# A local-attention and feed-forward kernel: score matmuls spread over both row halves and all column quarters, the down projection moved one slot on, and a new order on VectorE

## What is computed

```python
for i in range(DEPTH):                                   # 6
    x = attn_layer(shift_tokens(x), Wqkv[i], q_scale[i], k_scale[i], Wo[i]) + x
    x = ffn_layer(shift_tokens(x), ln_g[i], ln_b[i], W1[i], b1[i], W2[i], b2[i]) + x

# attn_layer: 16 heads of 64, window 32
q = l2norm(q) * qs ; k = l2norm(k) * ksc                 # then rotary with a scale
# local_attention: each window of 32 queries sees its own and the previous 32 keys
sim = einsum('bhwie,bhwje->bhwij', bq, bk2) * 8.0
attn = softmax(where(mask, -max, sim), -1)
out = einsum('bhwij,bhwje->bhwie', attn, bv2)

# ffn_layer: LayerNorm, 128 -> 2 x 341, a * gelu(gate), 341 -> 128
```

## Time and profile before

| what | us |
|---|---|
| median of three runs | 1690.2 (1688.54 to 1695.42) |
| the profiled execution | 1690.94 |
| its span, first to last instruction | 1689.1 |
| PE busy | 1604.0 (95%) |
| VectorE busy | 1461.7 (87%) |
| ScalarE busy | 1413.0 (84%) |
| GpSimd busy | 1312.3 (78%) |

### The profile page before, as it was taken

The page is one execution under the profiler, slowest core; times in us unless marked ns, Lnnn a source line. Parts: engine busy times, 40 slices in busy tenths (PEclk is TensorE's granted clock), DMA queues, the critical chain, the costliest instruction groups (busy, mean ns, idle before and its releaser), DMA issues.

```text
span 1689.1 us, 68758 instructions
## 1 busy us (share of the span) xinstructions
PE 1604.0 (95%) x25970; PEld 1294.4 (77%) x25970; DVE 1461.7 (87%) x3011; ACT 1413.0 (84%) x2851; POOL 1312.3 (78%) x1305
## 2 busy tenths in 40 slices
PE   7879999999999999999999999999999999999995
PEld 5667887777777778787777877777777777777773
DVE  4399998998899899889989989988998998889884
ACT  3267898988888898898888889888888988988885
POOL 6088888888788788888878888887888877777765
PEclk9799999999999999999999999999999999999997
DMA  4011111111111111111111111111111101110000
GB/s 150 31 43 40 36 38 38 31 45 31 53 34 31 37 37 39 50 36 33 31 37 43 48 39 31 33 31 50 45 36 37 31 28 39 40 33 26 28 24 26
DMA packets 41426, 66.40 MB, mean 39 GB/s; under 512 B 7072, under 2 KB 16032, under 8 KB 41376
## 3 DMA queue, kind: packets, MB, share of 16 engines
q1 hardware_dynamic: 40224, 65.38, 12.9%
q10 hardware_dynamic: 1152, 0.34, 0.1%
HBM read 20.61 MB, written 1.05 MB: 13 GB/s over the span
## 4 chain that ended last, share of the span: by engine, by line
PE 56%; ACT 28%; issue 10%; DVE 5%; ACTq 1%; DMA 0%; POOL 0%; DVEq 0%; POOLq 0%
PE ps_qs L530 12%; PE ps_q L530 8%; PE ps_a L530 7%; PE ps_tk L530 7%; PE ps_po L530 6%; PE ps_f L530 6%; PE ps_k L530 4%; PE ps_v L530 4%; ACT p_bd L942 4%; ACT L1052 3%; ACT L1049 3%; ACT prob L986 3%; ACT squares L948 3%; ACT q_t L942 3%; PE ps_po L650 2%
## 5 line engine op out<-in xcount | busy, mean ns | idle before, releaser
L419 POOL TENSOR_TENSOR qk<-qk,qk_rot 128x512 f32<-128x512 f32 x384 | 483.6, 1280 | 0.0
L427 POOL TENSOR_TENSOR qk<-qk,rnorm 128x512 f32<-128x512 f32 x384 | 393.0, 1044 | 77.2 <-DVE rnorm L1283 76.7
L434 POOL TENSOR_TENSOR prob<-prob,row_inv 128x512 f32<-128x512 f32 x192 | 200.4, 1044 | 152.7 <-DVE row_inv L1300 152.5
L1263 DVE TENSOR_REDUCE ssq<-squares 128x8 f32<-128x512 f32 x384 | 261.2, 680 | 3.6 <-ACT squares L948 3.4
L530 PE MATMUL ps_qs<-k_t,q_t 64*32 64x64 f32 x12224 | 210.5, 218 | 9.5 <-ACT ps_qs L942 9.4
L942 ACT COPY p_bd<-ps_po 64x512 f32<-64x512 f32 x378 | 217.1, 574 | 2.3
L530 PEld LDWEIGHTS ps_qs<-k_t,q_t 64*32 64x32 f32 x12224 | 179.8, 107 | 37.2 <-issue 27.8
L530 PEld LDWEIGHTS ps_po<-p_bd,v_back 128*64 128x64 f32 x3056 | 161.7, 137 | 46.0 <-issue 31.8
L530 PE MATMUL ps_po<-p_bd,v_back 128*64 128x64 f32 x3056 | 192.8, 225 | 0.0
L530 PE MATMUL ps_po<-p_bd,v_own 128*64 128x64 f32 x3056 | 188.5, 222 | 0.0
L530 PE MATMUL ps_a<-attn_t,wo_sb 128*64 128x257 f32 x1536 | 187.8, 386 | 0.0
(11 more groups left out here) (237 smaller groups left out, 4125.3 us busy)
## 6 DMA issues: line engine op xcount, KB each, us to landing
v_back<-v_own SPq DMA_DIRECT2D x192, 192.0 KB, 2.4
w_raw<-in_wqkv SPq DMA_DIRECT2D x48, 192.0 KB, 2.3
v_back<-v_own SPq DMA_DIRECT2D x96, 64.0 KB, 2.1
wo_sb<-in_wo SPq DMA_DIRECT2D x12, 256.0 KB, 3.0
w_sb<-in_w SPq DMA_DIRECT2D x6, 341.0 KB, 3.2
w_sb<-in_w SPq DMA_DIRECT2D x6, 192.0 KB, 2.7
x_in<-in_x SPq DMA_DIRECT2D x4, 256.0 KB, 4.4
out<-s_out SPq DMA_DIRECT2D x8, 128.0 KB, 1.9
```

Of the source, the lines that this page charges most:

```text
L419: nc.gpsimd.tensor_tensor(qk[:, s, i, :], qk[:, s, i, :], qk_rot[:, s, i, :], ALU.add).then_inc(added, 1)
L427: nc.gpsimd.tensor_tensor(heads(qk[:, s, i, :]), heads(qk[:, s, i, :]), rnorm[:, s, 8 * i:8 * i + 8].unsqueeze(2).to_broadcast([P, 8, HEAD ...
L434: nc.gpsimd.tensor_tensor(heads(prob[:, s, :]), heads(prob[:, s, :]), row_inv[:, s, :].unsqueeze(2).to_broadcast([P, 8, HEAD]), ALU.mult). ...
L1263: V.tensor_reduce(ssq[:, s, 8 * i:8 * i + 8], heads(squares[:, s, OCTET * i:OCTET * i + OCTET]), AX, ALU.add).then_inc(ssq_done, 1)
```

## The change

Three things are changed together.

**Scores in two banks.** `ps_q` and `ps_k` become halves of one two-bank tensor `ps_proj`, and `ps_qs` and `ps_tk` halves of another, `ps_score`. The scores of the first head of each pair go to the first bank and those of the second head to the second bank, 256 columns each. The column place is now `64 * odd + 32 * near`, where `near` tells two head pairs apart, so eight matmuls in a row use eight different pieces. `lay_mask` writes into both banks and therefore also waits for `k_turned`; the transposes of k wait for `sub_done`.

**Down projection.** `ff_down` moves from slot 1 (bank `ps_tk`) to slot 2, into columns 2 to 258 of the LayerNorm bank `ps_a`. The residual addition `after_ff` on VectorE moves from slot 2 to slot 3, and PE's wait for it moves from the transposes of slot 2 to the output projection of slot 3.

**VectorE's order.** The three Newton operations, the sums and the products are interleaved so that dependent operations are not neighbours. The last Newton operation, which writes `rnorm`, now stands behind the cosine product of q.

```diff
-        ps_q, ps_k, ps_v, ps_qs, ps_tk, ps_po, ps_a, ps_f = (
-            bank(n) for n in ("ps_q", "ps_k", "ps_v", "ps_qs", "ps_tk", "ps_po", "ps_a", "ps_f"))
+        ps_proj, ps_score = (ctx.enter_context(nc.psum_tensor(n, [P, 2, 512], F32)) for n in ("ps_proj", "ps_score"))
+        ps_q, ps_k, ps_qs, ps_tk = ps_proj[:, 0, :], ps_proj[:, 1, :], ps_score[:, 0, :], ps_score[:, 1, :]
+        ps_v, ps_po, ps_a, ps_f = (bank(n) for n in ("ps_v", "ps_po", "ps_a", "ps_f"))
+        ps_down = ps_a[:, TILES:TILES + SHIFTED]
...
-                ps, read = ((ps_qs, sub_done), (ps_tk, k_turned))[i]
-                wait(pe, read, u)
-                turn_into(ps, u, i, s)
+                wait(pe, sub_done, u)
+                turn_into((ps_qs, ps_tk)[i], u, i, s)
...
-                for c in range(PAIRS):
+                for far in range(2):
                     for half in range(2):
-                        g = 2 * c + half
+                        g = 2 * far + half
                         for odd in range(2):
                             w = 2 * half + odd
-                            for head in range(2):
-                                rows = slice(64 * head, 64 * head + 64)
-                                at = 64 * odd + WINDOW * head
-                                last = mm(ps[at:at + WINDOW, 64 * g:64 * g + 64],
...
+                            for near in range(2):
+                                c = 2 * far + near
+                                for head in range(2):
+                                    rows = slice(64 * head, 64 * head + 64)
+                                    at = 64 * odd + WINDOW * near
+                                    last = mm(ps[at:at + WINDOW, head, 64 * g:64 * g + 64],
...
-            def ff_down(u, m):
-
-                pe.wait_ge(k_turned, u + 1)
-                down_into(ps_tk, m)
+            def ff_down(m):
+
+                pe.wait_ge(centered, m + 3)
+                down_into(ps_down, m)
...
-                        if j == 2 and live_batch(n - 4):
-                            pe.wait_ge(x_ready, BATCHES + n - 3)
...
                     if j == 3:
                         if live_batch(n - 3):
                             ff_up(n - 3, 2)
+                        if live_batch(n - 4):
+                            pe.wait_ge(x_ready, BATCHES + n - 3)
                         if live_batch(n - 1):
                             out_projection(n - 1, 0)
                     if live(u - 4):
                         values(u - 4, n - 1, j, j % 2)
-                    if j == 1 and live_batch(n - 4):
-                        ff_down(u - 2, n - 4)
+                    if j == 2 and live_batch(n - 4):
+                        ff_down(n - 4)
...
                 act.wait_ge(q_turned, u + 1)
-                copy(ps_qs[:], mask_b[:, tile, :]).then_inc(mask_laid, 1)
+                act.wait_ge(k_turned, u + 1)
+                copy(ps_score[:, :, 0:OCTET // 2], mask_b[:, tile, :].rearrange("p (a b) -> p a b", a=2)).then_inc(mask_laid, 1)
...
-                    if j == 2 and live_batch(n - 4):
+                    if j == 3 and live_batch(n - 4):
                         after_ff(n - 4)
                     if j == 3 and live_batch(n - 2):
                         ln_var(n - 2)
                     if live(u - 3):
                         softmax_shift(u - 3, (j - 3) % 2)
                     if live(u - 1):
-                        newton(u - 1, (j - 1) % 2, u - 2)
+                        newton_half(u - 1, (j - 1) % 2)
                     sum_squares(u, 0, j % 2)
-                    rotate(n, j, 0)
+                    if live(u - 1):
+                        newton_square(u - 1, (j - 1) % 2)
+                    rotate_cos(n, j, 0)
+                    if live(u - 1):
+                        newton_finish(u - 1, (j - 1) % 2, u - 2)
+                    rotate_sin(n, j, 0)
                     if live(u - 3):
-                        sums(u - 3, (j - 3) % 2)
-                    rotate(n, j, 1)
+                        row_sums(u - 3, (j - 3) % 2)
                     sum_squares(u, 1, j % 2)
+                    if live(u - 3):
+                        invert_sums(u - 3, (j - 3) % 2)
+                    rotate_cos(n, j, 1)
+                    rotate_sin(n, j, 1)
```

More of the change, by code:

```diff
@@ L665, in project, with scores @@
                 mm(ps[:], xs_lo[:, toks], w_hi[:, cols], False, True).then_inc(done, 1)
-            def scores(u, j, s, ps=ps_qs, laid=True):
+            def scores(u, j, s, ps=ps_score, laid=True):
                 octet, tile = j // 2, j % 2
@@ L671, in scores @@
                 pe.wait_ge(k_turned, u + 1)
-                if ps is ps_qs and laid:
+                if laid:
                     pe.wait_ge(mask_laid, u + 1)
@@ L826, in drain @@
                 turn_into(ps_q, c, 0, 0)
-                pe.wait_ge(k_turned, c)
-                turn_into(ps_tk, c, 1, 0)
+                pe.wait_ge(k_scaled, END)
+                turn_into(ps_k, c, 1, 0)
                 out_projection(LAST - 1, 1)
[L830 to L834, removed]
+                pe.wait_ge(sub_done, b + 1)
+                turn_into(ps_qs, d, 0, 1)
+                scores(c, 2, 0, ps_proj, False)
+                turn_into(ps_tk, d, 1, 1)
                 values(a, LAST, 0, 0)
                 ln_spread(LAST - 2, END)
-                turn_p(b, 1, ps_tk)
+                pe.wait_ge(v_copied, END)
+                turn_p(b, 1, ps_v)
                 ln_mean(LAST - 1)
-                pe.wait_ge(sub_done, b + 1)
-                scores(d, 3, 1, ps_qs, False)
+                scores(d, 3, 1, ps_score, False)
                 ff_up(LAST - 2, 0)
@@ L847, in drain @@
                 ff_up(LAST - 2, 2)
-                values(c, LAST, 2, 0, ps_tk)
+                values(c, LAST, 2, 0, ps_k)
                 out_projection(LAST, 0)
-                turn_p(d, 1, ps_k)
+                turn_p(d, 1, ps_tk)
                 ln_spread(LAST - 1, END + 1)
@@ L1253, in rotate, with rotate_sin @@
                 cos = table[:, span(at, HEAD)]
-                sin = table[:, span(at + TILES * HEAD, HEAD)]
                 V.tensor_tensor(heads(qk[:, s, i, :]), heads(ps[:]),
                                 cos.unsqueeze(1).to_broadcast([P, 8, HEAD]), ALU.mult)
+            def rotate_sin(n, j, i):
+                s = j % 2
+                tile = j % 2
+                ps, scaled = ((ps_q, q_scaled), (ps_k, k_scaled))[i]
+                at = n // BATCHES * (4 * TILES * HEAD) + (2 * i * TILES + tile) * HEAD
+                sin = table[:, span(at + TILES * HEAD, HEAD)]
                 V.tensor_tensor(halves(qk_rot[:, s, i, :]), halves(ps[:])[:, :, ::-1, :],
@@ L1272, in clamp_unit, with newton_half @@
                 clamp(s)
-            def newton(c, s, used):
+            def newton_half(c, s):
                 dve.wait_ge(rn_started, c + 1)
@@ L1278, in newton, with newton_square, newton_finish @@
                                        op0=ALU.mult, op1=ALU.mult).then_inc(rn_step, 1)
+            def newton_square(c, s):
                 dve.wait_ge(rn_step, 2 * c + 1)
                 V.tensor_tensor(rn_b[:, s, :], rn_a[:, s, :], rn_0[:, s, :], ALU.mult).then_inc(rn_step, 1)
+            def newton_finish(c, s, used):
                 dve.wait_ge(rn_step, 2 * c + 2)
@@ L1416, in drain @@
                 newton(END + 1, 1, END)
-                after_ff(LAST - 1)
+                after_ff(LAST - 1, ps_tk)
                 ln_normalise(LAST)
@@ L1458, in score_masks @@
     seen = np.concatenate([k >= q, k <= q], 1)
-    m = np.where(seen, 0.0, MASKED)[None, None, :, None, None, None, :]
-    m = np.broadcast_to(m, (2, 2, WINDOW, TILES, PAIRS, 2, 2 * WINDOW)).copy()
-    m[0, :, :, 0, :, 0, 0:WINDOW] = MASKED
+    m = np.where(seen, 0.0, MASKED)[None, None, :, None, None, None, None, :]
+    m = np.broadcast_to(m, (2, 2, WINDOW, TILES, 2, PAIRS // 2, 2, 2 * WINDOW)).copy()
+    m[0, :, :, 0, :, :, 0, 0:WINDOW] = MASKED
     return m.reshape(P, TILES * 512).astype(np.float32)
```

52 lines of the change are left out of this document (32 added, 20 removed).

## The result

The changed kernel takes 1707.84 us (1704.43 to 1708.93, four runs) where the kernel before takes 1689.37 beside it: a ratio of 1.010, 95% interval 1.008 to 1.013. The forecast was 1683 with a range of 1665 to 1705. The profiled execution has a span of 1706.4 us, 17.3 more than before.

A forecast was written before the change was run, and what follows sets the result against it. ScalarE's list was taken to bound slots 0 and 1, PE's slots 2 and 3: -0.66 + 0.58 = -0.08 us a step, -3.4 us over 43 steps, with 3 early and 0.4 in the drain -6.8: 1683 us, range 1665 to 1705.

The forecast's parts named there:

- The loop of two parts: A step is ScalarE's list from slot 0's squares to slot 1's k copy, then PE's list through slots 2 and 3.
- The three blocks: Score blocks of slots 1, 2 and 3, put 0.39, 0.39 and 0.35 us shorter on the step's path.
- `rnorm`: Slot 0: ends at 818.05, not 815.45; LayerNorm factor's matmul 0.94 us later; ScalarE's attention copy in slot 1 loses 0.47 us.
- The rival in which `rnorm` is harmless: ScalarE does not wait for `rnorm`: -0.40 us a step, 1670 us with the ends; chance 0.22, all faster.
- The mask's wait: Slot 1: mask starts 0.68 us behind the k copy, 0.20 more than before (0.15 to 0.34); scores 0.22 behind the mask.
- The down projection: Moved into slot 2, it adds 1.32 us to PE's half of the step.
- `divide` and the rest of VectorE: At slot 2's start PE keeps about 1 us of cover for `divide`; the rest of VectorE's order costs nothing.
- The score block: Eight pieces give 8 rounds of 56 ns, not 16: each block saves 0.39 us (0 to 0.45), 0.63 us long.
- the loop's end: Slot 3's block saves only 0.35 us, because a shorter block hides less of the branch.
- the prediction's own price: Each 0.1 us that a score block keeps costs 0.3 us a step, 13 us in all.
- Ahead of the loop the term: Before the fifth step PE leads; 18 blocks x 0.39 bound the gain at 7 us, and 3 us is taken.
- The rival of blocks no faster: A score block stays at 1.02 us: +45 us, 1735 us; no or hardly faster blocks got chance 0.14 (slower 0.12).

## Why the prediction was wrong, by its own steps

- **The loop of two parts** was right. The three blocks, the move of the down projection and the late `rnorm` entered the step with the prices of that picture or close to them (0.40 for 0.40, +0.41 for +0.41, and in the kernel before a copy 0.54 us late for 0.47).
- **`rnorm`**, right: it ended 823.51 - 819.27 = 4.24 us into the step (4.25 put), the factor's matmul began at 4.37 (4.40 to 4.49 put), the attention copy at 7.99 (7.93). Between these two 3.62 us passed and not 3.48, so that part of the agreement is luck: an earlier start hid a longer way. The rival in which `rnorm` is harmless is out.
- **The mask's wait**, right: 0.70 us from copy to mask (0.68 put), 0.25 from its end to the scores (0.22).
- **The down projection**, right: slot 2 went from 7.03 us (its next projection started at 837.65 before) to 8.10, that is 1.32 less a block's 0.24.
- **`divide` and the rest of VectorE**, right: PE waits for nothing in slots 2 and 3.
- **The score block, the step that failed.** "Four starts fit in 24 ns ..., so eight fill at most 48 of the 56 ns and the issue keeps up" took the pace of four starts in a row for one that lasts for 64. It lasts for 32. A block saved 0.24 us, not 0.39. At the loop's end it saved 0.13, not 0.35: there I had no row for the sum, only the thought that a shorter block hides less of the branch, and the idle time there grew by 0.12 us (0.43 to 0.55) instead of 0.04. So the three terms were 0.15 + 0.15 + 0.22 = 0.52 us a step too good, of the 0.60 by which the step was missed. The other 0.08 is small change: slots 0 and 1 took 16.41 us for 16.16, 0.10 more than the block explains, of which 0.06 stands at the attention copy and 0.05 around the mask; slots 2 and 3 took 16.79 for 16.44, 0.02 less than the blocks explain. At the prediction's own price, 13 us for each 0.1 us that a block keeps, 0.15 is about 20 us, and the further 0.07 at the loop's end is 43 x 0.07 = 3: 1683 becomes 1706, and 1707.84 was measured. Ahead of the loop the term was about right: the sixth step, the first of the 43, starts at 221.55 us instead of 225.59, 4.0 earlier where 3 was put.
- **The rival of blocks no faster** had the right kind and too extreme a size: not 0 but 60% of the saving. Its sentence that from a saving under about 0.28 the kernel is slower by over 0.5% is what happened. The range should have been drawn through that point: I bounded a block between 0 and 0.45 and then closed the range at 1705, short of what half that saving costs.

The rule of the Trainium skill that was weighed (TensorE: Matmul & The Clock Gate, "Wait — 56ns, not 53.3ns?", no starts closer than about 25 ns) is not borne out after the change either: 64 starts in 0.64 us are 10 ns each. That the starts and not the pieces set the pace did come true, but only in the second half of a block, and at some 10 ns a start.

## What to carry to other kernels

Read the pace of an engine's starts over as long a run as the new code will ask for: a burst of four, or of 32, says nothing of 64. When work moves from one half of a loop to the other, price both halves and look which wait it had been hiding; here the down projection had covered the wait for the mask. And an instruction order that makes an engine less busy is worth nothing until that engine is the bound: with one operation put back, the new order on VectorE gained 0.76 us a step where VectorE was the bound and nothing in the changed kernel (32.82 for 32.84). That one operation, placed behind a long wait, cost 0.38 us a step there.

## What the runs showed of the hardware

- TensorE's matmul records on different pieces begin 7 ns apart for 32 records, then, after a stop of 0.08 us, some 10 ns apart. After 12 long matmuls the 7 ns are back, and in the doubled blocks after every pause of 0.07 us or more behind the 65th or 95th start. The Trainium skill gives about 4 ns of issue for each tile of a packed group (same page, "Part 3: Packing small matmuls — row/col tiling"); no run here shows that pace, nor does the section speak of the change behind 32.
- At the loop's branch PE was idle for 0.43 us behind 64 records at 14 ns, 0.55 behind 64 at 10 ns, and not at all behind 8 records of the output projection that take 1.0 us together.
- Doubling the score matmuls raised the instructions moved from 0.54 to 4.60 MB and PE's stand at a loop's end to 5.39 us. Whether the wait is for these instructions was not tried by itself.
